# A decoder layer on one core: token products and a bias added by accumulating DMAs, and the attention stage's DVE and ACT orders rewritten

## The reference, cut to what matters

```python
Xn  = layernorm(X, gamma, beta)
Q, K, V = split(Xn @ W_in + b_in, 3)
K, V = rotary(K), rotary(V)                  # first 256 features
A = sum(cos_sim(K) * cos_sim(V), over tokens) # one value per batch and feature
A = 0.5 * A + 0.5
Y = (A[:, None, :] * Q) @ W_out + b_out
x = layernorm(x + (Y + X))
```

## Time and profile before

| what | us |
|---|---|
| median of 3 runs | 876.67 |
| lowest and highest | 876.43, 882.21 |
| the profiled execution | 880.46 |
| its span | 878.6 |
| its mean granted PE clock | 0.967 of full speed |

### The profile page before, as it was taken

How to read it: one execution, slowest core, us unless ns; L and a number is a source line. 1 busy time by engine, 2 the same in 40 slices (tenths; PEclk the granted TensorE clock), 3 DMA queues, 4 the chain that set the end, 5 groups by cost and what they waited for, 6 DMA issues and landing times. The chain is left out here.

```text
span 878.6 us, 10788 instructions
## 1 busy us (share of the span) xinstructions
PE 810.3 (92%) x3698; PEld 659.9 (75%) x3702; DVE 695.5 (79%) x1329; ACT 298.4 (34%) x657; POOL 396.3 (45%) x307
## 2 busy tenths in 40 slices
PE   4799999999945889899999999999999999999995
PEld 3687887878832667588888888888887887887784
DVE  5766759388488787615676999999999999999997
ACT  4324424335115244222226333333333423423320
POOL 0503205015017344110326766777666776776431
PEclk9999999899985799999999999999999999999998
DMA  9440100125004222210012133132233323332113
GB/s 327 175 144 0 48 1 1 48 78 163 1 13 122 84 85 72 75 47 1 1 56 55 50 112 94 38 115 80 58 93 106 87 86 105 92 92 56 45 53 139
DMA packets 45672, 68.07 MB, mean 77 GB/s; under 512 B 17232, under 2 KB 26192, under 8 KB 45105
## 3 DMA queue, kind: packets, MB, share of 16 engines
q1 hardware_dynamic: 25456, 48.05, 16.3%
q0 software_dynamic: 18432, 18.80, 8.2%
q10 hardware_dynamic: 1728, 0.53, 0.3%
HBM read 107.29 MB, written 12.58 MB: 136 GB/s over the span
## 5 line engine op out<-in xcount | busy, mean ns | idle before, releaser
L1005 POOL TENSOR_TENSOR h_lo<-mid,h_hi 128x512 fp32r<-128x512 f32 x62 | 79.4, 1302 | 117.1 <-ACT h_hi L1125 112.2
L1026 POOL DMA_INDIRECT ctx_q<-table_dram,row_i x64 | 80.4, 1256 | 62.3 <-DVE xall L1350 41.3
L1135 ACT ACTIVATE gates<-dots 128x1 f32<-128x1 f32 x144 | 29.2, 203 | 232.1 <-DVE dots L1341 227.4
L1456 PE MATMUL gu<-x_hi,gate_hi 128*128 128x512 f32 x256 | 102.1, 399 | 3.1 <-DVE mid L1250 1.7
L1026 POOL DMA_INDIRECT scratch<-table_dram,row_i x64 | 82.7, 1292 | 39.5 <-issue 21.4
L1457 PE MATMUL gu<-x_lo,gate_hi 128*128 128x512 f32 x256 | 100.4, 392 | 0.0
L1458 PE MATMUL gu<-x_hi,gate_lo 128*128 128x512 f32 x256 | 100.4, 392 | 0.0
L1457 PE MATMUL gu<-x_lo,up_hi 128*128 128x512 f32 x256 | 99.6, 389 | 0.0
L1456 PE MATMUL gu<-x_hi,up_hi 128*128 128x512 f32 x256 | 99.6, 389 | 0.0
L1458 PE MATMUL gu<-x_hi,up_lo 128*128 128x512 f32 x256 | 99.6, 389 | 0.0
L1456 PE MATMUL ob<-down_hi,h_hi 128*128 128x512 f32 x248 | 97.6, 393 | 1.0 <-POOL h_lo L1005 1.0
(11 more groups left out here) (203 smaller groups left out, 1805.5 us busy)
## 6 DMA issues: line engine op xcount, KB each, us to landing
stage<-in_ctx SPq DMA_DIRECT2D x7, 1024.0 KB, 5.4
w_stage<-in_L_ffn_gate_w SPq DMA_DIRECT2D x8, 512.0 KB
w_stage<-in_L_ffn_up_w SPq DMA_DIRECT2D x8, 512.0 KB
w_stage<-in_L_ffn_down_w SPq DMA_DIRECT2D x8, 512.0 KB
x_dram<-xall SPq DMA_DIRECT2D x4, 1024.0 KB, 4.9
x_tok<-x_dram SPq DMA_DIRECT2D x16, 256.0 KB
out<-xall SPq DMA_DIRECT2D x8, 512.0 KB, 2.8
xall<-in_x SPq DMA_DIRECT2D x3, 1024.0 KB, 12.0
```

The lines of the kernel that those rows point to most:

```text
L1005: nc.gpsimd.tensor_tensor(lo[:, c], mid[c][:], hi[:, c].bitcast(F32), ALU.subtract).then_inc(hlo_done, 1)
L1026: nc.gpsimd.indirect_dma_start(rows[k], None, table_dram[:, :], bass.IndirectOffsetOnAxis(ap=row_i[t % 2][:, k:k + 1], axis=0), bounds_che ...
L1135: nc.scalar.activation(gates[:, t % 2, k:k + 1], dots[:, t % 2, k:k + 1], ACT.Silu).then_inc(gate_done, 1)
L1456: nc.tensor.matmul(dst, lhs[0], rhs[0], start=start, stop=False)
```

## The change

It does six things, all in the first block.

- `products` multiplies by the token weight itself (two `scalar_tensor_tensor` in place of two `tensor_tensor`) and so waits for `wgt_ready`. Tile 0 of a batch is written to a new buffer `total`, tiles 1 to 3 to the two `prod` buffers.
- POOL issues three accumulating DMAs a batch (`add_products`), which add 128 x 1024 fp32 from `prod` to `total`. Each waits for the landing of the one before it (`total_in`). `products(b, 3)` waits for the landing of the first.
- PE has one `token_sums` a batch, against a column of ones, that waits for the third landing. It stands between key_value 0 and 1 of the next batch, and for the last batch behind `attention(2, 0)`.
- The addition of b_out/2 to x is one accumulating DMA a batch, of 128 x 2048 fp32, at the end of POOL's work for the batch.
- The ctx maxima are taken one in batch 0 and three in batch 1. `gather_largest(0)` stands on PE ahead of the queries of batch 1, `spread(0)` behind the first of them. The quantising of all four parts lies in batches 2 and 3.
- At the start all of x is loaded from SP's queue, `normalise(0)` precedes the first `low_w`, and ACT and DVE alternate the slices of W_in with the slices of x.

```diff
 y_lo = sb("y_lo", [P, KC, S], F32R)
 kv = sb("kv", [P, 2, 2, D], F32)
+total = sb("total", [P, 2 * D], F32)
-cross = sb("cross", [P, ROT], F32)
-junk = sb("junk", [P, D], F32)
+junk = sb("junk", [P, D], BF16)
 trig = sb("trig", [P, TB, 2, P], F32)
 wgt = sb("wgt", [P, 2, 1], F32)
...
 sp.dma_start(xall[:, 0:2 * D], x_tiles[0][:, 0]).then_inc(x_half, 16)
...
+    pool.wait_ge(xhat_done, TB * (b + 1))
+    if b == 0:
+        pool.wait_ge(half_done, 1)
+    nc.gpsimd.dma_start(xall[:, b * TB * D:(b + 1) * TB * D].rearrange("p (t n) -> p t n", t=TB), half_bo[:].unsqueeze(1).broadcast_to([P, TB, D]),
+                        accum_op=ALU.add).then_inc(xb_in, 16)
 def weight(b, i):
     j = TB * b + i
     pool.wait_ge(sq_done, 2 * (j + 1))
     if j >= 2:
     own.did(nc.gpsimd.tensor_tensor(rnorm[:, i % 2], norm2[:, i % 2], neg_half[:, 0:2], ALU.pow))
     own.wait()
     nc.gpsimd.tensor_tensor(wgt[:, i % 2], rnorm[:, i % 2, 0:1], rnorm[:, i % 2, 1:2], ALU.mult).then_inc(wgt_ready, 1)
+
+    pool.wait_ge(prod_done, TB * b + i + 1)
+    if i > 1:
+        pool.wait_ge(total_in, 16 * (3 * b + i - 1))
+    nc.gpsimd.dma_start(total[:], prod[:, i % 2], accum_op=ALU.add).then_inc(total_in, 16)
 def z_rstd(b):
     pool.wait_ge(var2_ready, b + 1)
...
-    if b == 0:
-        pool.wait_ge(half_done, 1)
-    add_bias(b, (0, 1))
     weight(b, 1)
-    add_bias(b, (2, 3))
     weight(b, 2)
+    add_products(b, 1)
+    add_products(b, 2)
     weight(b, 3)
+    add_products(b, 3)
+    add_bias(b)
 z_rstd(2)
 for i in range(TB):
     pool.wait_ge(var2_ready, LAST + i + 1)
 def _(act):
...
 def copy_sums(b):
...
 high_w(0)
 high_w(1)
-high_w(2)
 act.wait_ge(gb_in, 32)
 high(0, 0)
+high_w(2)
+high(0, 1)
 high_w(3)
-for c in range(1, KC):
-    high(0, c)
+high(0, 2)
+high(0, 3)
 high_wq()
 for b in range(B):
     squares(b, 0)
+    if b:
+        copy_sums(b - 1)
     squares(b, 1)
     if b:
         for c in range(KC):
             high_y(b - 1, c)
     else:
         high_wo()
-    if b == 2:
-        ctx_scale(1)
-    if b == 3:
-        ctx_scale(3)
+    if b >= 2:
+        ctx_scale(2 * b - 3)
     squares(b, 2)
-    if b == 1:
-        ctx_scale(0)
+    query(b, 0)
+    query(b, 1)
     squares(b, 3)
-    for c in range(KC):
-        if c == KC - 1:
-            copy_sums(b)
-        query(b, c)
+    query(b, 2)
+    query(b, 3)
     if b < LAST:
         for c in range(KC):
             high(b + 1, c)
-    if b == 2:
-        ctx_scale(2)
+    if b in (1, 2):
+        ctx_scale(2 * b - 2)
+copy_sums(LAST)
 for c in range(KC):
     high_y(LAST, c)
...
 def products(b, i):
+
     j = TB * b + i
-    k_t, v_t = kv[:, i % 2, 0], kv[:, i % 2, 1]
-    both, cosp, sinp = prod[:, i % 2, 0:D], prod[:, i % 2, D:D + ROT], prod[:, i % 2, D + ROT:2 * D]
+    k_t, v_t, w_t = kv[:, i % 2, 0], kv[:, i % 2, 1], wgt[:, i % 2]
+    into = prod[:, i % 2] if i else total
+    both, cosp, sinp = into[:, 0:D], into[:, D:D + ROT], into[:, D + ROT:2 * D]
     dve.wait_ge(kv_out, j + 1)
-    if j:
-        dve.wait_ge(prod_done, j)
-    if j >= 2:
-        dve.wait_ge(asum_mm, j - 1)
-    own.did(nc.vector.tensor_tensor(both, k_t, v_t, ALU.mult))
-    own.did(nc.vector.tensor_tensor(cross[:].rearrange("p (n t) -> p n t", t=2), k_t[:, 0:ROT].rearrange("p (n t) -> p n t", t=2),
-                                    v_t[:, 0:ROT].rearrange("p (n t) -> p n t", t=2)[:, :, ::-1], ALU.mult))
+    dve.wait_ge(wgt_ready, j + 1)
+    if b:
+        dve.wait_ge(asum_mm, b)
+    if i == 3:
+        dve.wait_ge(total_in, 16 * (3 * b + 1))
+    own.did(nc.vector.scalar_tensor_tensor(both, k_t, w_t, v_t, ALU.mult, ALU.mult))
+    own.did(nc.vector.scalar_tensor_tensor(sinp.rearrange("p (n t) -> p n t", t=2), k_t[:, 0:ROT].rearrange("p (n t) -> p n t", t=2), w_t,
+                                           v_t[:, 0:ROT].rearrange("p (n t) -> p n t", t=2)[:, :, ::-1], ALU.mult, ALU.mult))
     own.wait()
     cos2 = trig[:, i, 0].unsqueeze(2).broadcast_to([P, P, 2])
     sin2 = trig[:, i, 1].unsqueeze(2).broadcast_to([P, P, 2])
     own.did(nc.vector.tensor_tensor(cosp.rearrange("p (n t) -> p n t", t=2), both[:, 0:ROT].rearrange("p (n t) -> p n t", t=2), cos2, ALU.mult))
-    nc.vector.tensor_tensor(sinp.rearrange("p (n t) -> p n t", t=2), cross[:].rearrange("p (n t) -> p n t", t=2), sin2, ALU.mult).then_inc(prod_done, 1)
+    nc.vector.tensor_tensor(sinp.rearrange("p (n t) -> p n t", t=2), sinp.rearrange("p (n t) -> p n t", t=2), sin2, ALU.mult).then_inc(prod_done, 1)
...
-    dve.wait_ge(xb_done, j + 1)
+    dve.wait_ge(xb_in, 16 * (b + 1))
...
 dve.wait_ge(x_in[0], 16)
 x_stats(0, (2, 3))
 x_variance(0)
-low_w(0)
 normalise(0)
-low_w(1)
-low(0, 0)
-low_w(2)
-low(0, 1)
-low_w(3)
-low(0, 2)
-low(0, 3)
-dve.wait_ge(hb_in, 16)
-nc.vector.tensor_scalar(half_bo[:], half_bo[:], 0.5, None, ALU.mult).then_inc(half_done, 1)
+for c in range(KC):
 for b in range(B):
+    if b >= 2:
+        ctx_quantise(2 * b - 4)
+    add_kv_bias(b, 0)
+    if b == 0:
+        add_kv_bias(b, 1)
+        low_wq()
+        products(b, 0)
+    if b < LAST:
+        next_stats(b + 1)
+    if b == 0:
+        dve.wait_ge(hb_in, 16)
+        nc.vector.tensor_scalar(half_bo[:], half_bo[:], 0.5, None, ALU.mult).then_inc(half_done, 1)
+    if b:
+        if b == 1:
+            ctx_amax(1)
+        add_kv_bias(b, 1)
+        products(b, 0)
+        multiplier(b - 1)
+        for c in range(KC):
+            low_y(b - 1, c)
+    if b < LAST:
+        normalise(b + 1)
     if b == 1:
+        ctx_amax(2)
+    add_kv_bias(b, 2)
+    products(b, 1)
+    if b == 0:
+        low_wo()
+    if b == 1:
+        ctx_amax(3)
         dve.wait_ge(c_amax, B)
         largest(amax_c[:])
-    if b == 3:
-        ctx_quantise(2)
+    if b >= 2:
+        ctx_quantise(2 * b - 3)
+    add_kv_bias(b, 3)
+    if b == 1:
+        scale_row(0)
+    products(b, 2)
+    if b == 0:
+        ctx_amax(0)
+    if b == 1:
+        scale_all(scale_c, 0)
     if b >= 2:
         for i in range(TB):
             finish_x1(b - 2, i)
-    add_kv_bias(b, 0)
-    if b == 1:
-        scale_row(0)
-    if b < LAST:
-        next_stats(b + 1)
-    if b == 0:
-        low_wq()
-    if b == 1:
-        scale_all(scale_c, 0)
-    add_kv_bias(b, 1)
-    products(b, 0)
-    if b:
-        multiplier(b - 1)
-        for c in range(KC):
-            low_y(b - 1, c)
-    else:
-        low_wo()
-        ctx_amax(0)
-    if b < LAST:
-        normalise(b + 1)
-    add_kv_bias(b, 2)
-    products(b, 1)
-    if b == 0:
-        ctx_amax(1)
-    if b == 2:
-        ctx_quantise(1)
-    if b == 3:
-        ctx_quantise(3)
-    add_kv_bias(b, 3)
-    products(b, 2)
-    if b == 0:
-        ctx_amax(2)
-    if b == 1:
-        ctx_quantise(0)
     products(b, 3)
-    if b == 0:
-        ctx_amax(3)
     if b < LAST:
         low(b + 1, 0)
         low(b + 1, 1)
...
-            pe.wait_ge(amul_done, b - 1)
+    elif b >= 2:
+        pe.wait_ge(amul_done, b - 1)
...
-def token_sums(b, i):
-    pe.wait_ge(prod_done, TB * b + i + 1)
-    pe.wait_ge(wgt_ready, TB * b + i + 1)
+def token_sums(b):
+    pe.wait_ge(total_in, 16 * 3 * (b + 1))
+    pe.wait_ge(prod_done, TB * b + 1)
     for c in range(8):
-        last = nc.tensor.matmul(ob[0][:, c:c + 1], prod[:, i % 2, c * P:(c + 1) * P], wgt[:, i % 2], start=(i == 0 and c == 0), stop=(i == TB - 1 and c == 7), skip_group_check=True)
+        last = nc.tensor.matmul(ob[0][:, c:c + 1], total[:, c * P:(c + 1) * P], ones_col[:], start=(c == 0), stop=(c == 7), skip_group_check=True)
     last.then_inc(asum_mm, 1)
...
 for b in range(B):
     if b:
         for k in range(KC):
             key_value(b, 0, k)
-        if b == 1:
-            gather_largest(0)
+        token_sums(b - 1)
         for k in range(KC):
             key_value(b, 1, k)
-        if b == 1:
-            spread(0)
-            pe.wait_ge(scale_done, 1)
         mix_sums(b - 1)
     for i in (2, 3):
         for k in range(KC):
             key_value(b, i, k)
-        token_sums(b, i - 2)
+    if b == 1:
+        pe.wait_ge(amul_done, 1)
+        gather_largest(0)
     for c in range(KC):
         query(b, c)
-        if c in (1, 2):
-            token_sums(b, c + 1)
+        if b == 1 and c == 0:
+            spread(0)
+    if b == 1:
+        pe.wait_ge(scale_done, 1)
     if b < LAST:
         transposes(b + 1, 0)
         transposes(b + 1, 1)
+    if b == LAST:
+        token_sums(LAST)
```

More of the change, by code:

```diff
@@ L173, in decoder_layer @@
             wgt = sb("wgt", [P, 2, 1], F32)
+            ones_col = sb("ones_col", [P, 1], F32)
             rsum = sb("rsum", [P, 8], F32)
@@ L189, in decoder_layer @@
             kv_mm, kv_out, sq_done, wgt_ready, prod_done, asum_mm = (sem(n) for n in ("kv_mm", "kv_out", "sq_done", "wgt_ready", "prod_done", "asum_mm"))
-            rsum_done, mix_mm, amul_done = sem("rsum_done"), sem("mix_mm"), sem("amul_done")
+            total_in, rsum_done, mix_mm, amul_done = sem("total_in"), sem("rsum_done"), sem("mix_mm"), sem("amul_done")
```

(32 more changed lines are left out.)

5 lines of the change are left out of this document (1 added, 4 removed).

## The result

| kernel | median, us | ratio to the kernel before, 95% interval | end of the attention stage, us |
|---|---|---|---|
| before | 879.44 | 1 | 257.69 |
| changed | 867.78 (864.76 to 868.05) | 0.9847 [0.9809, 0.9884] | 241.48 |
| changed, once more | 867.58 (864.33 to 869.47) | 0.9835 [0.9782, 0.9887] | 244.87 |

What follows compares the result with a forecast made beforehand. PE, busy 92% of the span, was taken as the bound. Gains of 37.5 us minus costs of 26.5 gave 11.0 less: 876.67 to 865.7 us median, range 854 to 881.

Steps and rivals of the forecast that it cites:

- `low(1,0)`: Batch 0: weight 3 queued behind the second DMA issue delays products(0,3); ready 54.1, PE wants it at 53.2: 0.9 us.
- `token_sums(0)`: Batch 0: third landing at 62.0, PE ready at 59.6; waits 2.4 us, plus 3.4 of clock.
- gather: Batch 1: PE, ahead of the queries, waits 6.9 us for DVE's largest, plus 3.4 of clock: 10.3.
- last batch's chain: Batch 3: three landings end at 210.8 (other limit, products(3,3): 203.4 + L), PE wants 205.1; 5.7 plus 3.4: 9.1 us.
- gains that follow: Attention stage: token sums 21.5, two block waits with clock 7.6 and 5.5, start 1.9, small waits 1.0: 37.5 us.
- The price of a block: Token sums on PE: 1.70 us between starts plus 0.09 refill, 1.79 us a block; 12 blocks go, 21.5 us.
- the start: Kernel start: transposes begin some 1.0 us earlier, first key_value 1.9 earlier; gain 1.9 us, or 1.5 if x comes later.
- The moved work on DVE: DVE's products: at most 0.2 us a tile added, beside PE; the 1.5 us collision with POOL's bias addition goes.
- L: Time from POOL's start on an accumulating DMA's issue to its landing: 6.3 us, bounds 4.1 and 12.1.
- rival of the short DMA: Accumulating DMAs with L of 4 to 5.5: batch 0 costs nothing, costs 17, time 856 us; chance 0.26 including clock holding.
- descriptors held back by `tensor_scalar`: POOL's DMA issues delayed by DVE: 1 us longer each gives L 7.3, 872 us; L 7.2 to 9, either cause, 0.18.
- The clock: PE waits over 2 us are followed by half-rate running (1.2 GHz level); 3.4 us lost, taken from two earlier waits.

Runs made afterwards that it cites:

- late-load run: Changed kernel, but SP issues the load of the second part of ctx only after the third landing of batch 0; 867.26 us, ratio 0.9830.
- two direct blocks: Changed kernel with late gather, weight(0,3) before batch 0's second DMA, and tile 3 summed by PE matmuls, not a DMA, in first and last batch; 852.59 us.
- the blocks apart: Kernel of the two direct blocks, with other PE work placed between the one-column matmul blocks in batches 0 and 3; 851.72 us, ratio 0.9656.

## Why the prediction was right, step by step

The costs as forecast and as the two profiles of the changed kernel show them, us. A cost is the wait plus what the clock took behind it; the clock's part is the time between starts against the same matmuls at the full rate (0.228 each and 0.1 of refill).

| place | forecast | first profile | second profile |
|---|---|---|---|
| `low(1,0)` | 0.9 | 2.07 + 2.9 = 5.0 | 1.98 + 1.6 = 3.6 |
| `token_sums(0)` | 2.4 + 3.4 = 5.8 | 0.7 | 2.26 + 3.3 = 5.6 |
| gather | 6.9 + 3.4 = 10.3 | 6.66 + 2.4 = 9.1 | 6.72 + 1.4 = 8.1 |
| last batch's chain | 5.7 + 3.4 = 9.1 | 3.88 + 3.3 = 7.2 | 3.85 + 3.1 = 7.0 |
| residual at the end | 0.4 | 0 | 0 |
| sum | 26.5 | 22.0 | 24.3 |
| stage | -11.0 | -16.2 | -12.8 |
| gains that follow | 37.5 | 38.2 | 37.1 |

- **Gains.** The last row is the stage's difference plus the costs, and it meets the forecast of 37.5 within 1 us in both profiles. No run takes the gains apart, so only their sum can be set against the forecast. The price of a block is confirmed where two follow each other: 126.77 to 128.56, 1.79 us. Inside the sum the start was over-sized: the first transposes come 0.8 us earlier, and the first key_value at 14.71 instead of 16.06, 1.35 instead of 1.9.
- **The moved work on DVE.** The products make no 1.5-us instruction any more; a tile costs 1.86 us of DVE's queue (52.63 to 54.49), and nothing on PE waited for it in batches 2 and 3. The estimate of nothing for this work holds there.
- **The gather.** The order of DVE's work that the forecast added up is in the trace line for line: four `low_y` 2.74, `normalise` 1.91, `ctx_amax` 2.28, the load, 1.97 of idle time, 2.29, each as long as in the earlier trace rows. Forecast 6.9, found 6.66; taken away with its clock, it gave 8.7.
- **L, the accumulating DMA.** The mis-sized term: 6.3 was taken, 5.0 of it from the load of 1 MB and 1.3 of issue; measured are 4.7 to the landing and 5.1 to the next issue. The issue takes 0.9, not the 1.3 to 1.4 of the earlier trace rows, and the rest 3.8. In the last batch the chain took 14.9 us instead of 18.9 (192.54 to 207.46); its third issue is put down to `products(3,3)`, the forecast's other limit, which came at about the same time as the second landing. The Trainium skill's price (DMA: Bandwidth & Descriptors, "Anatomy of one DMA — SWDGE (gpsimd) path"), as an estimate 3.2 us for 512 KB or 4.4 with the bytes counted twice, was below the measured 4.7 in both readings; the doubled one is close.
- **The case that came was not the forecast's.** The forecast took L of 5.5 to 7.2 (chance 0.42). A measured L of 4.7 to 5.1 belongs to its rival of the short DMA (4 to 5.5, chance 0.26), which had costs of 17 and a time of 856. Its costs at the gather and in the last batch came out about as written (9.1 and 7.2 against 10.3 and 6.4), but it had nothing for batch 0, where the two profiles show 5.7 and 9.2. The time is near the forecast and not near 856 because of that, in part.
- **Batch 0 came out near the forecast for another reason.** There the chain took 45.27 to 64.5, 19.3 us, which is 3 x 6.3 with a margin; but it was two short DMAs and one of 9 us that ran beside a 1 MB load. The forecast held the ctx load as something for DVE to wait for, and not as something that slows the DMA. The late-load run shows that it does: 5.1 us to the next issue instead of 9.2.
- **`low(1,0)`.** The forecast saw the queue (weight 3 behind the second issue, `low(1,0)` behind `products(0,3)`) but not the 1.4 us by which DVE's `low_wo` holds up POOL's weight 2, and with it the chain. A wait taken for 0.9 became 2.1 and brought the clock down. The Trainium skill has the rule (SBUF — State Buffer, "Who interferes with whom"): a DVE instruction with two SBUF inputs contends with a POOL instruction that reads SBUF. The trace agrees, 1.62 us beside L468 and 0.19 without. In batch 3 it happened again: 1.75 us, from 190.86, beside a two-input instruction of `ctx_quantise` that ends at 192.55, and the chain begins at 192.54 instead of the forecast 191.9. The part of that rule that the forecast had used as a rival, descriptors held back by `tensor_scalar`, does not show: the issue at 197.62 has two such instructions within 1.1 us of it and took 0.91, and the next issue came 5.1 us on.
- **The clock.** 3.4 us was taken for every fall; 1.4 to 3.3 were found. Part of a fall can lie in the wait itself: at the gather the clock was already at 0.68 in the stretch of 88 to 90 us, in which PE did nothing, and this fall cost 2.4 and 1.4, less than the one behind the last batch's chain (3.3 and 3.1).

So the mechanisms named were there, each wait at its place, and so were the gains; that the time was right to 2 us is partly luck. Against the first profile the sum of costs is 4.5 us too high: `low(1,0)` was 4.1 too low, `token_sums(0)` 5.1, the gather 1.2 and the last batch 1.9 too high. Against the second it is 2.2 too high, with errors of 2.7, 0.2, 2.2 and 2.1. An L that was too long and a wait at `low(1,0)` that was too short pulled in opposite directions. The sign given, a maximum over x some 11 us earlier, came as 16.2 and 12.8 us; the first of these is the profile of the fastest of the four runs (864.76 us).

One thing stays open. Waits of nearly the same length, 2.07 and 1.98 us for `low(1,0)` in the two profiles, were followed by falls of the clock that cost 2.9 and 1.6 us. In the second profile PE came to `token_sums(0)` 0.3 us earlier on the trace's clock, although it was 1.0 us behind ahead of `low(1,0)`. POOL's chain had begun those 1.0 us later (46.30, not 45.27) and taken 0.3 more, and the wait was 2.26 instead of 0.67. No run here tells what sets the length of a fall.

## What to carry to other kernels

Price a PE instruction that goes by the distance between starts, refill included, and then ask what the freed engine will wait for: here 37 us were gained and 22 to 24 given back at four places, of which 15 came back with PE's small instructions in a later place, weight 3 of batch 0 ahead of the second DMA and two direct blocks (852.6 us, 0.9666 of the kernel before; 851.7 with the blocks apart). A wait that ends with a landing grows by as much as is saved ahead of it on the same engine (0.67 us became 5.79 when 5.0 were saved), so linked waits are to be taken away together. And a chain of DMAs is priced with the loads that run beside it, not by its parts alone.

## What the hardware showed that was not expected

- Two blocks of one-column matmuls back to back, 3.5 us in which PE never idled, were followed by a granted clock of 0.50 to 0.58 (without any wait in the last batch of three kernels, and in batches 1 and 2 of a fourth). With twelve 512-column matmuls between them the clock stayed at 1.00 in the last batch; in batch 0 of the same kernel, with a wait of 0.63 us ahead of the first block, it fell to 0.50 between them.
- An accumulating DMA of 512 KB from SBUF to SBUF takes 4.7 us (median of twelve) and 8.4 to 9.0 when a 1 MB load of ctx is issued within 0.2 us of it, in nine profiles; with that load held back the twelve took 4.5 to 5.2, and with the load 1.9 us behind it the same DMA took 5.1. Later in the stage up to 6.4 was seen, where tile 3 is summed directly in every batch; no run tells why. The one of 1 MB whose source is 256 KB read four times takes 10.4 (median of four); in the whole stage DVE waited 1.1 us for it, once.
- A 128 x 1 multiplication on POOL takes 0.19 us, or up to 1.75 when DVE's two-input instruction of 2.3 us has begun before it; in the three cases of the first profile (43.71, 142.35 and 190.86) it ends within 0.1 us of DVE's end.
